# Layer 1's cross-attention begins in another order

## The reference

```python
x = x + _L1_xattn_ref(_layernorm(x), ctx_1024, ctx_1024, Wq, bq, Wk, bk, Wv, bv, Wo, bo)
# 16 heads of dimension 8; for each of the 8 batch elements b:
#   q = (LN(x[b]) @ Wq + bq) / sqrt(8)                     256 queries
#   k, v = ctx[b] @ Wk + bk, ctx[b] @ Wv + bv              1601 keys
#   softmax(q k^T) v, then @ Wo + bo
```

## Time and profile before

| | |
|---|---|
| median of three runs | 4132.2 us |
| profiled execution, its own time | 4135.38 us |
| its span | 4133.3 us |
| PE busy | 3852.2 us (93%) |
| DVE, ACT, POOL busy | 2639.5, 2665.9, 949.0 us |
| phase L1a begins | 371.4 us after the span's start |
| phase L1f begins | 1080.5 us |

### The profile page before, as it was taken

How to read it: one execution, slowest core, us unless ns; L and a number is a source line. 1 busy time by engine, 2 the same in 40 slices (tenths; PEclk the granted TensorE clock), 3 DMA queues, 4 the chain that set the end, 5 groups by cost and what they waited for, 6 DMA issues and landing times. The chain is left out here.

```text
span 4133.3 us, 71095 instructions
## 1 busy us (share of the span) xinstructions
PE 3852.2 (93%) x26053; PEld 2764.4 (67%) x26071; DVE 2639.5 (64%) x6105; ACT 2665.9 (64%) x4648; POOL 949.0 (23%) x842
## 2 busy tenths in 40 slices
PE   7898899999889999999999999978999999998885
PEld 6654444445467777777777777745888888886554
DVE  7655888888565666665665566556566666654762
ACT  6523577777447676767676676734777777776851
POOL 2100000000000000000000000001777777775433
PEclk9899999999899999999999999988999999999987
DMA  2100433322100000000000000010000000000012
GB/s 79 40 1 27 75 53 51 48 42 26 47 13 1 13 1 13 1 13 13 1 13 1 13 1 1 1 45 17 9 9 9 9 9 1 1 1 15 26 37 73
DMA packets 61040, 87.82 MB, mean 21 GB/s; under 512 B 13177, under 2 KB 51468, under 8 KB 59502
## 3 DMA queue, kind: packets, MB, share of 16 engines
q1 hardware_dynamic: 54729, 73.68, 8.0%
q10 hardware_dynamic: 4464, 6.30, 0.4%
q0 software_dynamic: 1504, 3.28, 0.2%
HBM read 58.07 MB, written 10.08 MB: 16 GB/s over the span
## 5 line engine op out<-in xcount | busy, mean ns | idle before, releaser
L2366 POOL TENSOR_TENSOR L3a_p_lo<-L3a_wq,L3a_p_hi 128x512 fp32r<-128x512 f32 (+1 forms) x480 | 626.3, 1320 | 207.5 <-ACT L3a_p_hi L2303 196.5
L1226 DVE CUSTOM_DVE_ANT_0 L2a_sc<-L2a_score,L2a_mask_n 128x804 f32<-128x804 f32 x512 | 500.0, 991 | 211.3 <-issue 194.4
L1116 ACT ACTIVATE L2a_pt<-L2a_ring 128x512 f32<-128x512 f32 x768 | 424.4, 597 | 138.2 <-PE L2a_ring L1005 133.1
L604 ACT ACTIVATE L1a_work<-L1a_ring 128x1024 f32<-128x1024 f32 x416 | 410.6, 1028 | 148.6 <-PE L1a_ring L436 147.9
L720 DVE TENSOR_REDUCE L1a_mx<-L1a_ring 128x2 f32<-128x1024 f32 x384 | 454.3, 1221 | 37.3 <-PE L1a_ring L455 31.9
L2458 DVE TENSOR_REDUCE L3a_mx<-L3a_ring 128x1 f32<-128x402 f32 (+2 forms) x640 | 322.8, 539 | 195.8 <-PE L3a_ring L2155 187.1
L1101 ACT ACTIVATE L2a_sc<-L2a_sc,L2a_nb 128x1608 f32<-128x1608 f32 x256 | 418.5, 1636 | 34.0 <-DVE L2a_nb L1231 34.0
L1005 PE MATMUL L2a_ring<-L2a_ident,L2a_sc 128*128 128x128 f32 x3072 | 424.5, 278 | 15.5 <-ACT L2a_sc L1101 9.1
L1005 PEld LDWEIGHTS L2a_ring<-L2a_ident,L2a_sc 128*128 128x128 f32 x3072 | 341.7, 141 | 86.0 <-issue 35.7
L2302 ACT ACTIVATE L3a_wq<-L3a_ring 128x512 f32<-128x512 f32 (+1 forms) x480 | 284.9, 594 | 159.2 <-PE L3a_ring L2077 113.0
L1020 PE MATMUL L2a_res<-L2a_pt,L2a_v 128*64 128x256 f32 (+1 forms) x3328 | 375.3, 382 | 1.4 <-ACT L2a_pt L1116 1.4
(11 more groups left out here) (744 smaller groups left out, 8196.7 us busy)
## 6 DMA issues: line engine op xcount, KB each, us to landing
L1a_keys<-L1a_k_hi SPq DMA_DIRECT2D x224, 52.0 KB
L1a_kt<-in_ctx_t SPq DMA_DIRECT2D x8, 800.5 KB, 4.5
L2a_ct<-in_ctx_t SPq DMA_DIRECT2D x8, 800.5 KB, 4.4
L1a_keys<-L1a_k_lo SPq DMA_DIRECT2D x112, 52.0 KB
L0a_cx<-in_ctx SPq DMA_DIRECT2D x16, 320.0 KB, 3.7
L3a_cx<-in_ctx SPq DMA_DIRECT2D x16, 320.0 KB, 3.6
L2a_mask_u<-in_mask SPq DMA_DIRECT2D x16, 200.1 KB, 4.5
L3f_sent<-in_L3f_blank SPq DMA_DIRECT2D x1, 3128.0 KB
```

The source lines that it names most:

```text
L604: act.activation(probs[:, (par * NU + u) % c.PS, :, :], ring[tile][:, :, :], ACT.Exp).then_inc(tile_free[tile], 1)
L1116: ins = act.activation(pt[:, t:t + 4, g // 3, q], bank[:, :].rearrange("p (t q) -> p t q", t=4), ACT.Copy)
L1226: dve.tensor_tensor_reduce(sc[:, two, e, w].rearrange("p (k j) -> p k j", k=2), score[e][:, :, 0:CH], mask_n[:, r % 2, w].rearrange("p (k ...
L2366: pool.tensor_tensor(p_lo[0:r, at % PL, 0:W], probs[0:r, at % 2, 0:W], p_hi[0:r, at % PH, 0:W].bitcast(F32), ALU.subtract).then_inc(part_o ...
```

## The change

1. The opening computes only group 0's keys (4 pieces) and between its first pieces one turn and the own queries; `first` names a PSUM bank for each of these 9 steps. It waits for 6 loads instead of 15 (the context of body 0 is loaded in two parts, and `wkr` is group 0's quarter); the other 9 have their own semaphore.
2. A list `LEAD` takes the place of the order at b = -1. Group 0's 14 maxima pieces start at once, and between them stand `late` steps on the bank `res`: late0 to late3 project all keys of body 0 once as high and low parts, late4 to late6 are the other three turns, late7 to late10 the query pieces, late11 the bias product.
3. The keys of groups 1 to 3 of body 0 are made by 36 DMA copies on SP, as for other bodies, behind four broadcasts of the constant rows. They stand ahead of the three puts of the queries. The maxima of these groups wait for them, and ACT's first key piece of body 1 waits for all 36, since it overwrites `k_hi`.
4. The first exponential waits for the last `late` query piece (the work area is shared).
5. The memset of `v`, the inverse root of the variance (one `pow` on 16 columns) and 12 of 16 normalisations go from DVE to POOL.

```diff
-def run_bodies(eng, order, steps):
+def run_bodies(eng, order, steps, lead=None):
     def body(b, par, offs):
-        for kind, off, n in order:
+        for kind, off, n in lead if lead and b == -1 else order:
...
+    LEAD = "T0 T3 T6 late0 T9 T1 late1 T4 T7 late2 value0 T10 T2 late3 T5 T8 late4 value1 T11 T12 late5 T13 late6 H value2 late7 U0 W late8 U1 value3 late9 U2 late10 U3 late11 U4"
...
-        wqr, wkr, bqr, bkr = sb("wqr", [P, NG, P]), sb("wkr", [P, NG, P]), sb("bqr", [P, NG]), sb("bkr", [P, NG])
+        wqr, wkr, bqr, bkr = sb("wqr", [P, NG, P]), sb("wkr", [P, P]), sb("bqr", [P, NG]), sb("bkr", [P, NG])
...
-        loads = [(ident, io["ident"]), (bkr, a("bkr")), (wkr, a("wkr")), (bqr, a("bqr")), (cols, io["cols"]), (wqr, a("wqr")),
-                 (wq, a("wq")), (bq, a("bq")), (wk, a("wk")), (bk, a("bk")), (wv, a("wv")), (bvg, a("bvg")), (wfin, a("wfin")),
-                 (pick, io["pick4"]), (bo, a("bo"))]
+        loads = [(wkr, a("wkr")[:, 0, :]), (cols, io["cols"]), (ident, io["ident"]), (bkr, a("bkr")), (bqr, a("bqr")), (wqr, a("wqr"))]
+        more_loads = [(wk, a("wk")), (bk, a("bk")), (wv, a("wv")), (wq, a("wq")), (wfin, a("wfin")), (bq, a("bq")), (bvg, a("bvg")),
+                      (pick, io["pick4"]), (bo, a("bo"))]
...
-        first = [("key", (0, k)) for k in range(KB)] + [("turn_x", k) for k in range(QC)]
-        first += [("key", (g, k)) for g in range(1, NG) for k in range(KB)] + [("own", g) for g in range(NG)]
-        first += [("query", k) for k in range(QC)]
-        first_at = lambda kind, n: first.index((kind, n))
-        first_bank = lambda kind, n: bank_of(first_at(kind, n) % (2 * c.RING))
+        first = {("key", 0): 2, ("turn_x", 0): 0, ("key", 1): 3, ("own", 0): 1, ("key", 2): 4, ("key", 3): 5,
+                 ("own", 1): 4, ("own", 2): 5, ("own", 3): 4}
+        first_at = lambda kind, n: list(first).index((kind, n))
+        first_bank = lambda kind, n: bank_of(first[kind, n])
+        cleared = lambda banks, k: max([i + 1 for i, bank in enumerate(list(first.values())[:k]) if bank in banks], default=0)
+        LK, LX = KB, KB + QC - 1
+        LQ = LX + QC
...
             held.clear_old(sp)
             load_context(1)
-            sp.wait_ge(ql_ok, QC)
+            sp.wait_ge(keys_ok, KB)
+            for r in range(4):
+                at = slice(32 * r + 3 * c.DH, 32 * r + 32)
+                sp.dma_start(keys[at, 0, 1:NG, :].bitcast(F32),
+                             keys[at, 0, 0:1, :].bitcast(F32).broadcast_to([c.DH, NG - 1, JP])).then_inc(same_in, 16)
+            sp.wait_ge(late_free, LK)
+            replicate_keys(0, range(1, NG))
+            sp.wait_ge(late_free, LQ)
             for copy, rows in enumerate((q_hi, q_hi, q_lo)):
                 sp.dma_start(scr_q[:, copy].rearrange("r d g j -> r (d g) j"), rows.bitcast(F32)).then_inc(q_put, 16)
             sp.wait_ge(q_put, 48)
             sp.wait_ge(blank_ok, 1)
+            sp.wait_ge(same_in, 64)
             for r in range(4):
                 at = slice(32 * r + 3 * c.DH, 32 * r + 32)
                 sp.dma_start(keys[at, 1, :, :].bitcast(F32), keys[at, 0, :, :].bitcast(F32)).then_inc(const_in, 16)
@@ -370,52 +398,44 @@
...
             pe.wait_ge(w_in, 16 * len(loads))
-            pe.wait_ge(c_got[0], 16)
             pe.wait_ge(zero_ok, 1)
-            for k in range(KB):
-                first_key(0, k)
-            pe.wait_ge(xn_ok, 1)
-            for k in range(QC):
-                first_turn_x(k)
+            first_key(0)
+            first_turn_x()
+            first_key(1)
+            pe.wait_ge(const_ok, 1)
+            first_own(0)
+            first_key(2)
+            first_key(3)
             for g in range(1, NG):
-                for k in range(KB):
-                    first_key(g, k)
-            pe.wait_ge(pre_free, first_at("turn_x", QC - 1) + 1)
-            for g in range(NG):
                 first_own(g)
-            for k in range(QC):
-                first_query(k)
-            for g in range(NG):
-                mm = pe.matmul(res[:, 0:1], wfin[:, g, :], bvg[:, g:g + 1], start=(g == 0), stop=(g == NG - 1))
-            mm.then_inc(bias_mm, 1)
-            pe.wait_ge(keys_ok, NG * KB)
-            pe.wait_ge(queries_ok, NG)
-            pe.wait_ge(ql_ok, QC)
+            pe.wait_ge(w_more, 16 * len(more_loads))
...
-                if n in c.opening and not (isinstance(b, int) and b == 0):
+                if b == 0 and g == 0:
+                    pe.wait_ge(queries_ok, 1)
+                    pe.wait_ge(keys_ok, ch + 1)
+                elif b == 0 and n in c.opening:
+                    pe.wait_ge(queries_ok, g + 1)
+                    pe.wait_ge(same_in, 64)
+                    pe.wait_ge(k_in[g], 192)
+                elif n in c.opening:
                     if g == 0:
                         pe.wait_ge(q_in, b * 64)
-                        if isinstance(b, int) and b == 1:
+                        if b == 1:
                             pe.wait_ge(const_in, 64)
-                    pe.wait_ge(k_in[g], b * 192)
+                    pe.wait_ge(k_in[g], (b + (g > 0)) * 192)
                 tile, before = c.ring.turn(b, "tops", n, c.RING)
-                if not (isinstance(before, int) and before == 0):
+                if before:
                     pe.wait_ge(tile_free[tile], before)
+                else:
+                    pe.wait_ge(pre_free, cleared([2 * tile, 2 * tile + 1], len(first)))
...
+            def late(b, par, k):
+                if b:
+                    return
+                if k:
+                    pe.wait_ge(late_free, k)
+                if k < LK:
+                    w = span_of(k)
+                    pe.matmul(res[:, 0:w.stop - w.start], wk[:, :], kt[:, 0, w], start=True, stop=True).then_inc(late_full, 1)
+                elif k < LX:
+                    n = k - LK + 1
+                    pe.wait_ge(xn_more, n)
+                    for t in range(4):
+                        mm = pe.transpose(res[:, t * P:(t + 1) * P], xn[:, 4 * n + t, :], ident[:, :])
+                    mm.then_inc(late_full, 1)
+                elif k < LQ:
+                    n = k - LX
+                    if n == 0:
+                        pe.wait_ge(more_ok, 1)
+                    pe.matmul(res[:, :], wq[:, :], yt[:, n * 512:(n + 1) * 512], start=True, stop=True).then_inc(late_full, 1)
+                else:
+                    for g in range(NG):
+                        mm = pe.matmul(res[:, 0:1], wfin[:, g, :], bvg[:, g:g + 1], start=(g == 0), stop=(g == NG - 1))
+                    mm.then_inc(late_full, 1)
...
+                if b == 0 and u == 0:
+                    act.wait_ge(late_full, LQ)
+                    act.wait_ge(keys_ok, KB)
+                    act.wait_ge(queries_ok, NG)
...
-                if k == 0 and not (isinstance(b, int) and b == 1):
-                    for g in range(NG):
-                        act.wait_ge(k_in[g], b * 192 - 192)
+                if k == 0:
+                    for g in range(0 if b > 1 else 1, NG):
+                        act.wait_ge(k_in[g], (b - (g == 0)) * 192)
...
+            pool.memset(half[:, :], -0.5)
+            pool.memset(v[:, :, :, :], 0.0)
+            pool.wait_ge(mv_ok, 1)
+            rsqrt_chunk(pool, st, half, slice(0, NT)).then_inc(rs_ok, 1)
+            for par in range(2):
+                ins = pool.memset(v[:, par, :, 0:c.H * c.VE].rearrange("p t (h e) -> p t h e", e=c.VE)[:, :, :, c.DH], 1.0)
+            ins.then_inc(v_ok, 1)
+            pool.drain()
+            for n in range(1, QC):
+                for t in range(4 * n, 4 * n + 4):
+                    ins = pool.tensor_scalar(xn[:, t, :], x[:, t, :], st["mv"][:, t, 0:1], st["rs"][:, t:t + 1], ALU.subtract, ALU.mult)
+                ins.then_inc(xn_more, 1)
             pool.memset(one[:, :], 1.0)
...
+            dve.tensor_scalar(wq[:, :], wq[:, :], scale, None, ALU.mult)
+            dve.tensor_scalar(bq[:, :], bq[:, :], scale, None, ALU.mult)
+            dve.tensor_copy(ident_b[:, :], ident[:, :]).then_inc(more_ok, 1)
+
+            def late(b, par, k):
+                if b:
+                    return
+                if k < LK:
+                    w = span_of(k)
+                    dve.wait_ge(late_hi, k + 1)
+                    dve.scalar_tensor_tensor(k_lo[:, w], res[:, 0:w.stop - w.start], bk[:, 0:1], k_hi[:, w].bitcast(F32),
+                                             ALU.add, ALU.subtract).then_inc(late_free, 1)
+                elif LX <= k < LQ:
+                    w = slice((k - LX) * 512, (k - LX + 1) * 512)
+                    dve.wait_ge(late_hi, LK + k - LX + 1)
+                    dve.scalar_tensor_tensor(q_lo[:, w], res[:, :], bq[:, 0:1], q_hi[:, w].bitcast(F32), ALU.add,
+                                             ALU.subtract).then_inc(late_free, 1)
 
```

(40 more changed lines are left out.)

145 lines of the change are left out of this document (80 added, 65 removed).

## The result

| | before | after |
|---|---|---|
| median, same chip | 4133.47 us (4131.21 to 4134.99, 5 runs) | 4153.99 us (4150.11 to 4160.38, 5 runs) |
| profiled execution: own time, span | 4135.38, 4133.3 us | 4154.61, 4152.8 us |
| phase `L1a`, first instruction to `L1f`'s first | 709.1 us | 727.6 us |

The account below looks back on a forecast made before the run. TensorE, busy 93% of the span, was taken as the bound, so its standstills are paid in full. +14.2 us wait at body 1 and +1.5 clock make +15.7: 4148 us on the median, range 4137 to 4158.

Parts of the forecast that it names:

- The opening: Layer 1's start up to the first maxima: first reduce at 394.0, 27.3 us before 421.26; late3 done at 408.4.
- SP's queue: 36 copies ahead of the query puts take 32.9 us; puts start 22.9 us later, at 441.3, everything behind moves equally.
- U0 of body 1: Group 0's first maxima piece waits on PE for its key copies: 495.99 to 510.2, +14.2 us (+11.7 to +22.9).
- The landing: Group 0's body 1 copies land 2.5 us after the twelfth's issue, within 0 to 11.2: at 510.2.
- The fixed cost of about 2 us: Skill rule for each DMA transfer, mostly completion: landing 2 and not 2.5 us behind issue, an estimate of 4147.
- Rival B: Key-copy waits don't bind at body 1's first maxima piece, the first exponential's 10 us stay: 4122, chance 0.08.
- C: Body 0's copies on SP run at 0.71 us each, queue shifts 15.6: +8.4 us, 4141, chance 0.14.
- D: Both waits longer, late3 as late as 411 and landing at its upper bound: +27 us, 4159, chance 0.08.
- The clock: PE at half clock for at most 6 us after its standstill at body 1: +1.5 us, within 0 to 3.
- "There is neither a second loss nor a return.": Later groups and body 2 get key copies in time, body 2's with 30 us to spare: 0 us.
- the prediction's own sign: Distance from body 1's first maxima piece to the end of the layer should stay as before.
- "Were they gone, these are what gives the 10 us": Opening savings (memsets, normalisations, smaller loads) cost nothing while the key-copy waits stand; without those waits they give 10 us.

Follow-up runs that it names:

- The experiment with 12 copies: Kernel before, with 12 extra key copies to unread scratch on SP's queue in front of the puts of the queries: 4145.97 us, ratio 1.0033.
- two buffers: Changed kernel with two buffers for the projected high and low key rows, so ACT waits for the body before the last: 4153.39 us, ratio 1.0040.
- the second traces: Unedited kernels profiled once more: before 4138.53 us own time (layer 709.1), after 4161.06 us (layer 727.9).
- the old order with wide puts: Kernel before, each put of the queries cut into four of 32 rows: 4136.72 us, ratio 1.0007.

## Why the prediction was nearly right, and where it was not

The mechanism was the predicted one: SP's queue is shifted as a whole, and PE waits at U0 of body 1. The result is 6.0 us above the forecast and inside the range. Of these 6.0 us, 2.9 lie in the layer (+18.6 for +15.7), 2.0 outside it (the medians differ by 20.5 and the layers by 18.5), where nothing was changed, and 1.3 in the base: the kernel before has a median of 4133.47 in five runs, and the forecast started from 4132.2. Point by point, in the order of the prediction:

- *The opening.* PE started at 375.3 (predicted 377), the root on POOL took 2.93 us (3.3), the first reduce came at 392.95 (394.0), late3 ended at 407.1 (408.4). The first exponential was at 436.9 and not at 434; this changed nothing.
- *SP's queue.* 36 copies took 32.4 us, 0.90 each (32.9, 0.913 by the earlier trace rows). The puts started 21.2 us later (22.9), puts to landing 33.7 us (34.3), what follows them to the first of body 1's copies 20.5 (20.7). Cut so that 32 rows stand outermost, the same bytes took 14.8 us. The mean busy share of the 16 DMA engines was 0.26 in the first case and 0.83 in the second, about 4 and 13 engines. The rule of the Trainium skill (DMA: Bandwidth & Descriptors, section "Why a DMA increments its semaphore by 16 and not by 1"), by which the slowest dimension sets the number of engines, agrees with the two shares.
- *The landing.* The twelfth copy's issue ended at about 505.1 and PE went on at 508.49: 3.4 us, where I took 2.5 within 0 to 11.2. Three such places give 3.4 to 4.3 us. The fixed cost of about 2 us that the prediction set beside it stands in the Trainium skill (DMA: Bandwidth & Descriptors, section "Anatomy of one DMA — SWDGE (gpsimd) path") for transfers issued from GpSimd. These come from SP, and took longer. The landing is one of the few terms that had no row, and its 0.9 us too few stand against 2.6 us by which the copies were issued earlier than I had worked out.
- *U0 of body 1.* At 508.49 (510.2). The layer itself began 1.3 us earlier in this execution (370.17 against 371.44), so that is +13.8 us in the layer's own time (+14.2). Rival B, that this wait doesn't bind, fell with the wait of 14.7 us; C, a pace of 0.71 us, with the 0.90; D, that late3 and the landing are both late, with 407.1 and 3.4 us. The time alone would not have told: 4154.0 is 5.0 us from D's 4159 and 6.0 from the forecast, for another reason.
- *The clock.* Over the 6 us behind the wait it was 0.67 (1.00 in the same 6 us before); the piece up to the first point is 1.9 us longer (1.5):

```profile
508.50:514.50 6.00, 6.00 (x39) 3.75 (x40) 3.29 (x6) 2.77 (x7) 0.00 (x0) 0.67 0.47 56
```

- *"There is neither a second loss nor a return."* This is the step that failed. By the prediction's own sign the distance from U0 of body 1 to the end of the layer had to be as before; it was 589.3 us and not 584.5. I looked at who needs body 2's keys, with 30 us to spare, and not at what body 2's first key piece overwrites: `k_hi`, from which 32 of body 1's 48 copies read (the other 16 read `k_lo`). With a landing of 3.4 to 4.3 us behind the last issue there was about a microsecond to spare before, when the issue ended at 517.7 and the key piece ran at 522.67:

```profile
516.71 1.00 SPq L329 DMA_DIRECT2D L1a_keys<-L1a_k_hi  x1
...
522.67 0.69 ACT L620 ACTIVATE L1a_k_hi<-L1a_aux,L1a_bk 128x512 fp32r<-128x512 f32 x1
```

  After, the issue of the last one ended at 537.23, 19.5 us later, the piece ran at 541.53 and ACT had waited 4.6 us, PE behind it 3.8; with PE's slower pace behind that, this part of the layer is 6.9 us longer. The code has this wait for body 2 before and after the change (ACT's first key piece waits for the copies of the body before), and I used it for body 1 only. The experiment with 12 copies shows it in the old order (5.1 us beside a wait of PE of 3.5), and two buffers take it away: the middle piece is 18.6 us again, as in every trace without this wait.
- *The return.* 4.0 us come back over the later bodies, and only 1.6 in the second traces (542.7 against 544.3), where the middle piece is 5.2 longer and not 6.9. It isn't the waits that bring it: the old order with wide puts has no long wait and its last piece is 3.4 us shorter too. What does is open.
- *What is gained.* "Were they gone, these are what gives the 10 us": with both waits taken away the first exponential is 10.1 us earlier and the layer 8.6 us shorter than before, of which the wide puts may account for 1.8.

In sum: +13.8 and +1.9 for +14.2 and +1.5, which is the predicted mechanism and its size, and the net +2.9 of the second wait and the return, for 0. That this net is small is luck: the second wait cost 6.9 us, and 4.0 came back for a reason that the prediction did not have.

## What to carry to other kernels

Work put on an in-order DMA queue was paid here where the last transfer behind it was needed: follow that queue to its end, and for each transfer ask both who reads its target and who overwrites its source. A start that is made earlier on the compute engines is worth only as much as the queue that feeds the next stage lets through; here the new order was +18.5 us with narrow puts and one buffer. With wide puts in both orders it gave nothing (707.6 against 707.4), and with two buffers as well it was 6.9 us better than the old order with wide puts. When an effect is under 10 us in 4 ms, measure the stage in the trace and not only the whole.

## What the runs showed of the hardware that was not expected

- A store of 3 MB in three transfers with 4 rows outermost took 33.7 us at a DMA share of 0.26, in twelve with 32 rows outermost 14.8 us at 0.83, of which 11.7 us are the 12 issues themselves.
- After the last issue of a set of copies of 8 rows between partitions had ended, the engine that waited for them went on 3.4 to 4.3 us later (439.54 to 442.99, 505.1 to 508.49, 537.23 to 541.53), each time with further transfers issued behind them.
- POOL took 0.95 us for a normalisation of 128x128 (11.37 us for 12), DVE 0.26 in the kernel before (4.19 for 16) and 0.35 in the changed one (1.41 for 4).
- `L3s`, whose code is unchanged, differed by 5 to 7 us between two executions of one kernel, and its granted clock with it (0.71 and 0.74 against 0.87 and 0.90 over the same 40 us).
